# GpSimd makes the upper halves of V's and O's weights, and the first steps of attention stand in a new order

## The reference, cut to what matters

```python
# x, ctx: (16, 256, 512) float32; 16 heads of 32; INNER = 1536
h = layernorm(x)
q, k, v = h @ Wq.T + bq, ctx @ Wk.T + bk, ctx @ Wv.T + bv    # 16 heads of 32
q, k = rope(q), rope(k)
p = softmax(causal(q @ k.T / sqrt(32)))
x = x + (p @ v) @ Wo.T + bo                                   # attention
x = x + ffn(layernorm(x))      # 4-bit weights in blocks of 32, 16-bit steps for every activation
```

## The kernel before, in words

| step | engine, line | what it does |
|---|---|---|
| bn | DVE, L502 | mean and variance of a half of x |
| stat | POOL, L388 to L392 | 1/sqrt(variance) and shift of one item, four linked operations |
| xn | ACT, L628 | x normalised |
| XT, xthi, xtlo | PE L743, ACT L632, DVE L507 | x transposed; upper and lower half |
| cthi, ctlo | ACT L641, DVE L512 | halves of the context |
| sumw, sumc | ACT, L605 | sums of magnitudes of a weight, of a context |
| MX, scale | PE L726, DVE L451 to L469 | totals; powers of two |
| hi, lo | ACT L624, DVE L497 | halves of the weights. 0 to 3: Q and K in two pieces each; 4: V; 5: O |
| QK, raw, rope | PE L707, ACT L649 and L652, DVE L521 to L526 | q and k of a group; read out of PSUM; rotated |
| V, Vev | PE L707, ACT L676 | v of half of the keys; read out |
| S, max, exps, recip | PE L776 to L781, DVE L529 and L530, ACT L658, DVE L534 | scores, row maxima, exponentials with sums, reciprocals |
| norm | POOL, L432 and L434 | probabilities times reciprocals, two products |
| PT, pte | PE L792 and L797, ACT L665 and L668 | probabilities transposed; read out |
| PV, othi, otlo | PE L808, ACT L672, DVE L545 | heads' outputs and their halves |

## Time and profile before

### The profile page before, as it was taken

How to read it: one execution, slowest core, us unless ns; L and a number is a source line. 1 busy time by engine, 2 the same in 40 slices (tenths; PEclk the granted TensorE clock), 3 DMA queues, 4 the chain that set the end, 5 groups by cost and what they waited for, 6 DMA issues and landing times.

```text
span 1531.4 us, 24407 instructions
## 1 busy us (share of the span) xinstructions
PE 1378.5 (90%) x9198; PEld 775.2 (51%) x9198; DVE 1185.7 (77%) x1794; ACT 966.0 (63%) x2030; POOL 340.1 (22%) x325
## 2 busy tenths in 40 slices
PE   4899999999999999969999998999999106999998
PEld 3566676666666666634444443444444002444443
DVE  6778888888888888748878885888899798566541
ACT  6788888888988888754422223999788784212210
POOL 1354455554545454420111110000000000000000
PEclk9899999999999999979999999999999657999999
DMA  6111111111121211132333333666689999666522
GB/s 245 39 56 56 63 70 61 62 67 70 70 84 70 70 56 56 35 106 109 129 108 128 117 117 117 233 243 247 236 308 329 414 411 367 217 212 223 197 96 83
DMA packets 93413, 228.94 MB, mean 149 GB/s; under 512 B 8560, under 2 KB 8688, under 8 KB 90352
## 3 DMA queue, kind: packets, MB, share of 16 engines
q1 hardware_dynamic: 92288, 220.04, 40.4%
q10 hardware_dynamic: 1008, 7.34, 1.2%
HBM read 144.51 MB, written 82.84 MB: 148 GB/s over the span
## 4 chain that ended last, share of the span: by engine, by line
PE 32%; DVE 8%; ACT 6%; DMA 5%; issue 3%; SPq 0%; POOL 0%; ACTq 0%; DVEq 0%
PE ffn_banks L1233 16%; PE ffn_banks L1218 16%; DVE qg L1518 3%; ACT qg L1329 2%; DMA ffn_ring<-gates_dram 2%; DVE ffn_peaks L1414 2%; DMA ffn_wide<-ups_dram 1%; DMA signs_dram<-qg 1%; ACT ffn_rest L1277 1%; ACT ffn_ring L1333 1%; DVE ffn_rest L1516 1%; DMA ffn_ring<-ups_dram 1%; DVE ffn_ring L1501 1%; ACT ffn_wide L1358 1%; DVE ffn_rest L1500 0%
## 5 line engine op out<-in xcount | busy, mean ns | idle before, releaser
L1218 PE MATMUL ffn_banks<-ffn_wide,ffn_rest 128*128 128x512 f16 x2304 | 502.3, 381 | 8.0 <-DVE ffn_rest L1452 4.3
L1218 PEld LDWEIGHTS ffn_banks<-ffn_wide,ffn_rest 128*128 128x128 f16 x2304 | 226.0, 98 | 284.1 <-issue 14.0
L1233 PE MATMUL ffn_banks<-ffn_rest,ffn_wide 128*128 128x512 f16 x1152 | 251.5, 382 | 83.0 <-DVE ffn_wide L1557 83.0
L1233 PEld LDWEIGHTS ffn_banks<-ffn_rest,ffn_wide 128*128 128x128 f16 x1152 | 113.2, 98 | 221.2 <-issue 87.0
L658 ACT ACTIVATE qg<-score_banks,neg_max 128x128 f32<-128x128 f32 (+1 forms) x512 | 208.0, 452 | 18.3 <-DVE neg_max L530 18.3
L1368 ACT ACTIVATE ffn_u_steps<-ffn_ring,ffn_scales 128x1024 int16<-128x1024 f32 x48 | 55.1, 1148 | 158.8 <-DMA ffn_ring<-ups_dram 146.5
L1277 ACT ACTIVATE ffn_rest<-ffn_banks,ffn_row_back 128x1024 f32<-128x1024 f32 x72 | 79.5, 1105 | 108.8 <-PE ffn_banks L1218 97.1
L432 POOL TENSOR_TENSOR qg<-qg,per_sum 128x512 f32<-128x512 f32 x64 | 82.5, 1290 | 270.2 <-DVE per_sum L534 270.2
L434 POOL TENSOR_TENSOR qg<-qg,per_sum 128x1024 f32<-128x1024 f32 x64 | 134.0, 2094 | 0.0
L658 ACT ACTIVATION_READ_ACCUMULATOR qg<-score_banks,neg_max 128x1 f32 x512 | 122.5, 240 | 0.0
L665 ACT ACTIVATE pt<-ring_banks 128x512 f32<-128x512 f32 x128 | 70.5, 614 | 48.2 <-PE ring_banks L792 47.2
(11 more groups left out here) (194 smaller groups left out, 2691.4 us busy)
## 6 DMA issues: line engine op xcount, KB each, us to landing
ups_dram<-ffn_rest SPq DMA_DIRECT2D x48, 512.0 KB, 3.8
ffn_ring<-ups_dram SPq DMA_DIRECT2D x48, 512.0 KB, 5.6
gates_dram<-ffn_rest SPq DMA_DIRECT2D x24, 512.0 KB, 2.8
ffn_ring<-gates_dram SPq DMA_DIRECT2D x24, 512.0 KB, 4.5
signs_dram<-qg SPq DMA_DIRECT2D x24, 512.0 KB, 4.1
ffn_wide<-ups_dram SPq DMA_DIRECT2D x12, 1024.0 KB, 17.5
qg<-signs_dram SPq DMA_DIRECT2D x24, 512.0 KB, 10.4
ffn_rest<-w_parts_dram SPq DMA_DIRECT2D x36, 256.0 KB, 4.1
```

The lines of the kernel that those rows point to most:

```text
L1218: last = pe.matmul(banks[:, pair_of(s), half, :], w[:, m % 2, wp, c, :], xq[:, xp, n, c, :], start=(k == 0), stop=(k == 3 * DC - 1))
L1233: last = pe.matmul(down_banks[:, g % 2, t, :], oq[:, g % 2, op, m, t * P:(t + 1) * P], w_down[:, wp, wk, c], start=(start and k == 0), sto ...
```

## The change

Steps hi4 and hi5, the upper halves of V's and O's weights (2048 elements per partition each), leave ACT's plan and enter GpSimd's: hi4 between stat+1 and norm0, hi5 between norm0 and stat+2. They wait for scale1 and count in a semaphore of their own, `vo_hi_ready`, for which lo4 and lo5 now wait; the declared but unused semaphore `up_scaled` is dropped. The four plans of the beginning are ordered anew. Among what moves: on PE MX1 ahead of MX2, XT0+1 ahead of S1, XT0+2 and MX3 earlier; on ACT sumw0 ahead of xn0, hi1 ahead of hi0, hi3 ahead of hi2, raw0 ahead of sumc+1, sumw3 ahead of sumw2, cthi+1, sumc+2 and sumc+3 to right behind exps0, raw3 ahead of exps1; on DVE rope0 ahead of the two bn+1, scale1 ahead of scale2, bn0+2 behind max1 and the ctlo+1 ahead of the xtlo+1, lo5 ahead of rope0+1. The lines for the later items are as before.

```diff
-PE_BEGIN = ("MX0 XT0 XT1 QK0 QK1 S0 MX2 MX1 QK2 V1 S1 XT0+1 XT1+1 QK3 V0 QK0+1 PT0 S2 PV0 PT1 QK1+1 S3 PV1 XT0+2 "
-            "XT1+2 MX3 PT2 QK2+1 V0+1 PV2")
-ACT_BEGIN = ("xn0 xn1 sumw0 sumw1 xthi0 hi0 cthi1 cthi0 xthi1 hi1 hi2 hi3 sumc+1 raw0 sumw2 sumw3 raw1 xn1+1 xn0+1 "
-             "exps0 hi4 raw2 Vev1 xthi0+1 xthi1+1 hi5 cthi1+1 cthi0+1 exps1 raw3 Vev0 raw0+1 pte0 xn0+2 sumc+2 "
-             "othi0 sumc+3 exps2 pte1 xn1+2 raw1+1 othi1 xthi0+2 xthi1+2 exps3 pte2 cthi0+2 xn1+3 raw2+1 othi2 "
-             "cthi1+2")
-DVE_BEGIN = ("bn0 bn1 rs dsum0 dsum1 scale0 xtlo0 lo0 ctlo1 ctlo0 xtlo1 lo1 bn1+1 lo2 lo3 bn0+1 rope0 max0 scale2 "
-             "scale1 rope1 recip0 bn0+2 lo4 max1 xtlo1+1 xtlo0+1 bn1+2 ctlo1+1 ctlo0+1 rope2 recip1 rope3 max2 "
-             "otlo0 rope0+1 lo5 recip2 max3 otlo1 xtlo0+2 xtlo1+2 scale3 bn0+3 bn1+3 recip3 rope1+1 ctlo0+2")
-POOL_BEGIN = "stat+1 norm0 stat+2 norm1 norm2"
+PE_BEGIN = ("MX0 XT0 XT1 QK0 QK1 S0 MX1 MX2 QK2 V1 XT0+1 S1 XT1+1 QK3 V0 QK0+1 PT0 S2 PV0 PT1 QK1+1 S3 XT0+2 PV1 "
+            "MX3 XT1+2 PT2 QK2+1 V0+1 PV2")
+ACT_BEGIN = ("sumw0 xn0 sumw1 xn1 xthi0 hi1 hi0 xthi1 cthi0 cthi1 hi3 hi2 raw0 sumc+1 sumw3 sumw2 raw1 xn0+1 xn1+1 "
+             "exps0 cthi0+1 sumc+2 raw2 cthi1+1 sumc+3 xthi0+1 Vev1 xthi1+1 raw3 exps1 Vev0 raw0+1 pte0 xn0+2 "
+             "othi0 exps2 pte1 xn1+2 xthi0+2 raw1+1 othi1 xthi1+2 exps3 pte2 cthi0+2 xn1+3 raw2+1 cthi1+2 othi2")
+DVE_BEGIN = ("bn1 bn0 rs dsum0 dsum1 scale0 xtlo0 lo1 lo0 xtlo1 ctlo0 ctlo1 lo3 lo2 rope0 bn0+1 bn1+1 max0 scale1 "
+             "scale2 rope1 recip0 lo4 max1 ctlo0+1 ctlo1+1 xtlo0+1 bn1+2 xtlo1+1 bn0+2 rope2 recip1 rope3 max2 "
+             "otlo0 lo5 rope0+1 recip2 max3 xtlo0+2 otlo1 xtlo1+2 scale3 bn1+3 bn0+3 recip3 rope1+1 ctlo0+2")
+POOL_BEGIN = "stat+1 hi4 norm0 hi5 stat+2 norm1 norm2"
...
+                if name == "hi":
+                    m, cols = PARTS[g]
+                    pool.wait_ge(scaled, DVE_COUNT["scale", 1, 0])
+                    w_col = (Q_COL, K_COL, V_COL, O_COL)[m]
+                    pool.tensor_scalar(attn_hi[:, m, :, cols], raw_w[:, m, :, cols], inv[:, w_col:w_col + 1], None,
+                                       ALU.mult).then_inc(vo_hi_ready, 1)
...
-                    dve.wait_ge(hi_ready, ACT_COUNT["hi", g, 0])
+                    if g < 4:
+                        dve.wait_ge(hi_ready, ACT_COUNT["hi", g, 0])
+                    else:
+                        dve.wait_ge(vo_hi_ready, POOL_COUNT["hi", g, 0])
```

More of the change, by code:

```diff
@@ L276, in attend @@
         scaled = sem("scaled")
-        hi_ready, lo_ready = sem("hi_ready"), sem("lo_ready")
+        hi_ready, vo_hi_ready, lo_ready = sem("hi_ready"), sem("vo_hi_ready"), sem("lo_ready")
         x2_stored = sem("x2_stored")
@@ L967, in feed_forward @@
         w_hi, w_split = sem("w_hi"), sem("w_split")
-        up_raw_in, up_summed, up_joined, up_scaled = sem("up_raw_in"), sem("up_summed"), sem("up_joined"), sem("up_scaled")
+        up_raw_in, up_summed, up_joined = sem("up_raw_in"), sem("up_summed"), sem("up_joined")
         parts_stored = [sem(f"parts_stored{b}") for b in range(2)]
```

## The result

The changed kernel takes 1536.93 us in the median of 20 executions (1534.36 to 1539.3), the kernel before 1534.35 in the median of 20 beside it (1531.43 to 1536.0). The ratio is 1.0018, 95% interval 1.0011 to 1.0025, which is 2.8 us slower (1.7 to 3.8); the medians themselves lie 2.6 apart. The forecast was 0.6 us faster, with a range up to 1536.5.

What follows compares the result with a forecast made beforehand. TensorE's waits for lower weight halves, chiefly 6.4 us before V1, were taken as what an order could win. V1 -0.9, V1 to max1 0, max1 to recip2 +0.3 gave -0.6 us: 1533.7 us, range 1530.3 to 1536.5 (8 in 10).

Steps and rivals of the forecast that it cites:

- The first 26 us cost nothing: Opening: reordered sumw0, hi1 and hi3 stand between the same ends; cost 0, at most 0.3 us late.
- Five sums, MX1, scale1: Before hi4: five ACT sums end at 32.5, MX1 needs 0.9 us more, scale1 is done at 34.6.
- bn, stat, xn, exps0: Behind rope0: bn steps end at 31.2, stat+1 by 33.8, and exps0 begins near 35.0 instead of 33.67.
- hi4 on GpSimd: V's upper weight halves on GpSimd: 2.0 us, between 1.9 and 3.6, ending at 36.7.
- The prediction's estimate of 1.8 to 1.9 us: hi4 on GpSimd by a skill page's roughly line-rate one-input rule, putting V1 0.1 to 0.2 us earlier than the sum.
- The slow-hi4 rival: hi4 on GpSimd takes 4.9 us, delaying rope1, recip0, lo4 and V1 one for one: 1537.3 us; chance 0.10.
- rope1 waits, lo4 goes ahead of norm0 and runs alone: DVE before V1: rope1 waits for hi4's end, lo4 runs 39.5 to 41.85, V1 begins 0.9 us earlier.
- V1 to max1, 7.0 us: From V1's start to max1's: again 7.0 us, 1.5 less to 0.7 more; max1 starts at 49.0.
- max1 to recip2: DVE-bound stretch: bn0+2 adds 0.9 us, a 0.6 pause before rope3 goes; +0.3 us.
- at recip2, so it stays: After recip2 the order is as before and nearly all TensorE, so the 0.6 us gain there remains.
- The port rule of "SBUF — State Buffer": GpSimd and DVE operations, two-port or with two SBUF inputs, block each other for whole instructions; scale2 might delay V1 0.8 us.

Runs made afterwards that it cites:

- e7: The kernel before with eight GpSimd operations of 1024 elements per partition added in its idle first microseconds, to time GpSimd's forms; total time not compared.
- e12: The changed kernel run again as it is, beside the kernel before; 1536.89 us, ratio 1.0031 to the kernel before.
- e11: The changed kernel with XT0+1 back behind S1 on TensorE; 1533.62 us, ratio 1.0005 to the kernel before.
- e10: e4's order with hi4 moved to GpSimd as a two-input product, hi5 staying on ACT; 1525.89 us, ratio 0.9956 to the kernel before.
- e1: The kernel before, in its old order, with only hi4 and hi5 moved to GpSimd; 1535.65 us, ratio 1.0019 to the kernel before.
- e2: The changed kernel's new order with hi4 and hi5 back on ACT; 1537.24 us, ratio 1.0023 to the kernel before.
- e3: The changed kernel with hi4 cut in two, half on GpSimd and half on ACT; 1533.41 us, ratio 0.9992 to the kernel before.
- e8: The changed kernel with sumc+1 again ahead of raw0 and both bn+1 steps ahead of rope0; 1533.82 us, ratio 1.0004 to the kernel before.
- e4: The kernel before, both hi steps on ACT, with V's sums, MX1, scale1, hi4 and lo4 pulled forward; 1523.13 us, ratio 0.9937 to the kernel before.
- e9: The changed kernel with hi4 and hi5 on GpSimd as two-input products instead of the scalar form; 1536.63 us, ratio 1.0030 to the kernel before.

## Why the prediction was wrong

By its own steps, in the profiled execution:

- *The first 26 us cost nothing*: as forecast. raw0 begins at 25.88, where it began at 25.80 before. DVE had its pause ahead of rope0 (2.48 us), in which the bn steps would have fitted.
- *Five sums, MX1, scale1*: the direction was right, the size 0.9 us short. The sums end at 32.8, not 32.5; MX1 then takes 1.5 us until scale1 begins at 34.31, not 0.9 (the granted clock was 0.63 in 32 to 34), and scale1 is done at 35.54, not 34.6.
- *bn, stat, xn, exps0*: right. exps0 begins at 35.00. It is the fifth sum ahead of raw1 that sets this and not the bn steps: stat+1 is done at 33.03, before ACT gets to xn+1 at 33.59.
- *hi4 on GpSimd*: **the step that failed.** It was taken at 2.0 us between ends of 1.9 and 3.6 and measured 5.46, beyond both. The reason given, half of a two-input product because one input is read, is what a copy costs (1.04 us for 1024 elements in e7) but not what the scalar form costs (2.85). The prediction's estimate of 1.8 to 1.9 us, by a one-input rate, fails with it. The slow-hi4 rival, at 4.9 us and 1537.3, came nearest and had 0.10; that its rule, one for one, gives 2.9 us over before at 5.46 is luck, since it counts hi4's whole duration. For V1 the number that mattered was the time for which the ports are held: 3.66 us (35.65 to 39.31), 1.7 more than the 2.0 taken.
- *rope1 waits, lo4 goes ahead of norm0 and runs alone*: right in every link. 0.9 (scale1) and 1.7 (hold) are the 2.6 us by which rope1 began late (39.31 for 36.7), and V1 came 2.45 us later than forecast.
- *V1 to max1, 7.0 us*: 7.2.
- *max1 to recip2*: forecast 19.9, measured 18.3. max1 is 1.7 us late against before and recip2 only 0.4: DVE had no pauses left there, and rope3's two products ran at 1.23 and 0.69 us, where they took 1.63 and 1.49 before, while norm1 on GpSimd was held up instead (2.04 and 2.39 us for 1.04 and 1.89). This was no lasting gain. norm1 ended at 64.75, PT1 waited for it (1.2 us in the waits above), and at batch item 1 the whole is late by 1.2 to 1.3 us, and by 1.4 at 15.1. The step "at recip2, so it stays" was wrong as well: the shift that lasts is read on TensorE, not on DVE.
- *The rest of the 2.8 us* is not seen in the first profile, whose span is 1.2 us longer. The drop behind 1.2 that e12 shows costs 1.7 us, and 1.2 and 1.7 together are about what was measured. That the changed kernel meets this drop more often fits the counts given under e12, but rests on single profiles and is not shown. A second place varies too: from 15.1 to 15.3 the profiled executions take 17.3 us (e11, e10), 18.9 (before), 20.6 (changed) or some 22 (e12 and most others, the faster kernels among them), by how long the clock stays at its lower level there (mean granted clock in 642 to 654: 1.00 in e11, 0.86 before, 0.72 changed, 0.57 in e12). Part of that is given back right behind: the first product with O's weights at the end of attention begins 3.2 us late in the changed kernel (664.39 for 661.22) and 5.6 in e12 (666.77), whose spans are 1.2 and 3.7 us longer. These differences are not tied to the edits.

The port rule of "SBUF — State Buffer" (section "SBUF: two separate sides") in the Trainium skill, weighed ahead of the result, holds for the two-input operations, which waited. The one-input steps of scale2 did not wait, but they are of one element. In e7 a one-input step of three elements took 0.88 us beside the beginning of the immediate form (the line at 17.32; 0.17 before), so the rule's other kind, a two-port mode, may be at work there; no run separates it. The rule does not hold in that hi4 keeps the ports for its whole instruction: DVE went on 1.8 us before hi4's end.

Of the two theories tried, neither stands alone. Each half of the change by itself is shown to delay V1 to 44.4 (e1, e2), with exps0's and the sums' lateness on the one side and the ports on the other. Easing the ports in the changed kernel brings its time back to before (e3, 0.9992); easing the sums brings V1 1.0 us forward and likely does the same for the time (e8, 1.0004).

## What to carry to other kernels

An idle engine is no free place: ask what the moved step costs there, in that very form, and what its ports shut out meanwhile, and if no row shows the form, measure it before ordering other steps around it. Pauses ahead of a critical read are the cheapest place for work, so look which step's inputs are there early enough: putting V's sums there and pulling the steps behind them forward (e4) gave 9.7 us, where the change lost 2.8. Do not take a gain or loss at one engine's step for the end's: look for the same shift on the bounding engine an item later, and again at the end of the part, since some of it can still go (e3: 2.2 us at 1.3, 0.7 at 15.1).

## What the runs showed of the hardware

- GpSimd's scalar multiply is slower than its two-input multiply: 5.46 us against 3.60 for 2048 elements from float32 to float16 (the changed kernel, e9). For 1024 elements into float16 it takes 2.85 us, or 2.77 with an immediate, while a copy into float16 takes 1.04 and a fill 0.95 (e7).
- Its scalar form lets DVE go early. Two-input operations on DVE resumed 3.66 us after the start of a 5.46 us instruction and 1.0 us after the start of a 2.86 us one, in both cases 1.8 us before its end (the changed kernel, e3); in e1 it was 1.9. The two-input product of 3.60 us kept them out to within 0.1 us of its end (e9).
- A DVE operation on a single element per partition is held up as long as a large one if both inputs are in SBUF: 3.18 us for 0.16 (the changed kernel). A one-input operation can be held up as well: 0.88 us for 0.17 with three elements (e7), but none of one element was.
- The same wait of 1.7 us of TensorE, at the same place in batch item 1, was followed by a clock of 0.50 in e12 and of 1.00 in the first profile of the same kernel; the stretch from 1.2 to 1.3 took 1.7 us longer.
